# Gate, up and key-value products of an attention and mixture-of-experts block as three rounded products of split operands

## The chip, the cores and the metric

The kernel runs on one core of one Trainium2 chip. The metric is device microseconds of one launch, the median of several runs. The engines are TensorE (PE; PEld is its weight load), VectorE (DVE), ScalarE (ACT), GpSimd (POOL) and SyncE (SP), which issues most of the DMA.

## The reference

One block over x of 8 x 512 tokens of width 256: a modulated layer norm, multi-head latent attention with 16 heads, a gated residual, a second modulated norm, a shared gated feed-forward part of inner width 352, and 16 experts of inner width 176 with capacity 128 and top 4. Cut to what the change touches:

```python
h = _layernorm(x, axis=-1) * (1 + ca) + sa
fused = hidden @ w_kv_a                      # 192 query-latent, 64 key-latent, 64 rotary columns
...
h = _layernorm(x, axis=-1) * (1 + cb) + sb
scores = jax.nn.softmax(x @ gate_w.T, axis=-1)
topk_w, topk_i = jax.lax.top_k(scores, K)
...
shared = jax.nn.silu(x @ sw_gate) * (x @ sw_up) @ sw_down
```

All is f32.

## The kernel before

Eight batches of 512 tokens (4 tiles of 128) run in one loop. A batch has eight head pairs. `step` is one head pair: scores, exponentials, transposes of the probabilities, values, and the query projection of the next pair. Between two batches stands `middle(b, n, post, pre)`: `post` is the end of batch b (output projection, residual x1, second norm h2, shared feed-forward part, router), `pre` the start of batch n = b + 1 (key-value part, absorbed keys, first query projection). Seven of these have both halves; batch 0 starts with `pre` alone after the weights are prepared, and batch 7 ends with `post` alone, followed by the experts. Every engine has its own program, in an order written out by hand, and they meet at semaphores. GpSimd scatters routing entries, multiplies and adds the modulation of h2 (lines 494 and 496, behind a wait for the query rotation at line 493), and copies x.

The normed h1 is turned by TensorE (`turn_h1`, two halves of the width, both through bank 6 of the accumulator, the second after ScalarE has emptied the first). ScalarE writes hT with scale and bias (`turned_h1`, line 1043). The key-value part is `PS[t] = hT^T wkva_sb` for four tiles and two halves of the width (line 831), in the order 2, 0, 1, 3, each behind a wait for its bank. ScalarE then sums squares, GpSimd takes roots, VectorE scales into qn and kmat.

h2 is turned in two parts: three tiles (`turn_h2`, written by `turned_h2`, line 1050), then the last (`turn_h2_last`, `turned_h2_last`, line 1056). The inner width of the shared part is in three slices. The third slice, 96 columns, carries the 16 router columns too: `ffn_router` (lines 793 and 795), part 0 for the first 384 tokens and part 1 for the last 128. `ffn` (lines 781 and 783) computes gate and up of slices 0 and 1. `tanh_gate` on ScalarE and `silu_mid` on VectorE finish each slice.

The query projection and the scores already use split operands: a value is written once rounded to fp32r by ScalarE (high), VectorE subtracts that from the full value (low), and three products, high x high, low x high and high x low, are added in one bank (`scores`, lines 650 to 652; `q_project`; `q_low` at line 1262). The tiles hT, h2T, wkva_sb, sg_sb (gate and router columns) and su_sb (up) are f32.

## Time and profile before

| | us |
|---|---|
| median of 3 timed runs | 1249.4 |
| lowest, highest | 1245.29, 1251.21 |
| the profiled execution | 1254.99 |
| its span, first to last instruction | 1253.1 |

The profile is one execution. Its timelines give start and length in us, the engine, the line, what was written from what, and in square brackets how long the engine stood idle before and what released it. "x4" joins neighbouring records of the same form. A matmul's length holds a fixed latency and overlaps the next one, so its cost is the distance from one start to the next.

### The profile page before, as it was taken

The page shows a single profiled execution, that of the slowest core. Times are in us where ns is not written, and L with a number is a line of the kernel's source. Part 1 is how long each engine was busy: PE and PEld are TensorE (multiplying, and loading weights), DVE is VectorE, ACT ScalarE, POOL GpSimd, SP SyncE. Part 2 cuts the span into 40 slices and gives each one's busy share as a digit, 9 for nine tenths or more (in the row PEclk, how much of TensorE's full clock was granted, in tenths as well). Part 3 has the DMA queues.
Part 4 walks back from the last instruction along what each step waited for, and adds up shares of the span by engine and source line. Part 5 has one row for each costly group of instructions (what it writes and reads, how often), then busy time and mean ns, then how long its engine had stood idle before and what let it go on. Part 6 is the DMA issues. An engine that isn't in the chain of part 4 may idle for free.

```text
span 1253.1 us, 26074 instructions
## 1 busy us (share of the span) xinstructions
PE 1177.9 (94%) x7620; PEld 953.2 (76%) x7620; DVE 836.0 (67%) x2581; ACT 667.2 (53%) x1920; POOL 276.5 (22%) x332
## 2 busy tenths in 40 slices
PE   6799999999999999999999999999999999996782
PEld 3688778887888778887888778877888778873441
DVE  3677568776777667775877677766877577756221
ACT  2476626663567536763576447663667356731220
POOL 1000122211221122113212131212221122102553
PEclk9999999999999999999999999999999999997977
DMA  9410001000200001000100001000100010004752
GB/s 304 142 57 0 1 18 51 0 0 0 67 0 0 0 17 50 0 0 11 56 0 0 0 17 50 0 0 17 50 0 0 0 50 1 0 1 136 210 129 38
DMA packets 48317, 46.17 MB, mean 37 GB/s; under 512 B 10048, under 2 KB 44960, under 8 KB 48296
## 3 DMA queue, kind: packets, MB, share of 16 engines
q1 hardware_dynamic: 29096, 30.90, 8.1%
q0 software_dynamic: 7168, 6.37, 2.8%
q10 hardware_dynamic: 12032, 8.65, 2.4%
q8 instruction: 10, 0.16, 0.1%
q14 instruction: 11, 0.09, 0.0%
HBM read 35.04 MB, written 15.11 MB: 40 GB/s over the span
## 4 chain that ended last, share of the span: by engine, by line
PE 84%; DMA 5%; DVE 4%; issue 2%; ACT 2%; SPq 1%; POOL 1%; POOLq 0%; DVEq 0%; ACTq 0%
PE PS L671 11%; PE PS L692 10%; PE PS L802 8%; PE PS L650 7%; PE PS L651 6%; PE PS L652 6%; DMA out<-x_res,toku 5%; PE PS L636 4%; PE PS L810 4%; PE PS L831 3%; PE PS L623 3%; PE PS L626 2%; PE PS L627 2%; PE PS L624 2%; PE PS L625 2%; PE PS L781 2%
## 5 line engine op out<-in xcount | busy, mean ns | idle before, releaser
L987 ACT ACTIVATE probs<-probs,nmax 128x512 f32<-128x512 f32 (+3 forms) x512 | 283.0, 554 | 124.5 <-DVE nmax L1231 121.5
L1231 DVE CUSTOM_DVE_ANT_0 probs<-PS,cmask 128x512 f32<-128x512 f32 (+3 forms) x512 | 229.3, 488 | 98.6 <-PE PS L652 96.2
L540 POOL DMA_INDIRECT tab_dram<-entry,slot x112 | 110.5, 986 | 392.4 <-PE PS L692 371.1
L650 PE MATMUL PS<-kTh,qTh 128*128 128x512 f32 (+3 forms) x512 | 177.5, 347 | 1.7 <-DVE qTl L1262 1.5
L651 PE MATMUL PS<-kTl,qTh 128*128 128x512 f32 (+3 forms) x512 | 164.9, 322 | 0.0
L652 PE MATMUL PS<-kTh,qTl 128*128 128x512 f32 (+3 forms) x512 | 164.9, 322 | 0.0
L996 ACT ACTIVATE pT<-PS 128x384 f32<-128x384 f32 (+3 forms) x320 | 127.3, 462 | 70.6 <-PE PS L671 70.5
L671 PE MATMUL PS<-ident,probs 128*128 128x128 f32 x1280 | 164.8, 275 | 0.0
L692 PE MATMUL PS<-pT,kmat 128*64 128x512 f32 (+3 forms) x1024 | 151.9, 439 | 0.3 <-issue 0.3
L671 PEld LDWEIGHTS PS<-ident,probs 128*128 128x128 f32 x1280 | 141.4, 140 | 10.3 <-issue 7.4
L692 PEld LDWEIGHTS PS<-pT,kmat 128*64 128x64 f32 x1024 | 68.0, 136 | 76.0 <-issue 62.1
L802 PE MATMUL PS<-wvo,oT 128*128 128x256 f32 x512 | 116.4, 381 | 0.0
L1262 DVE TENSOR_TENSOR qTl<-PS,qTh 128x512 fp32r<-128x512 f32 x128 | 87.1, 685 | 34.0 <-ACT qTh L982 34.0
L650 PEld LDWEIGHTS PS<-kTh,qTh 128*128 128x128 f32 x512 | 96.5, 188 | 13.2 <-issue 4.6
L802 PEld LDWEIGHTS PS<-wvo,oT 128*128 128x128 f32 x512 | 95.4, 190 | 13.7 <-issue 1.4
L1248 DVE COPY pT<-PS 128x512 f32<-128x512 f32 (+2 forms) x192 | 81.5, 462 | 31.7 <-PE PS L671 31.4
L652 PEld LDWEIGHTS PS<-kTh,qTl 128*128 128x128 f32 x512 | 96.7, 189 | 5.4
L651 PEld LDWEIGHTS PS<-kTl,qTh 128*128 128x128 f32 x512 | 96.9, 189 | 4.9 <-issue 1.7
L987 ACT ACTIVATION_READ_ACCUMULATOR probs<-probs,nmax 128x1 f32 x512 | 95.7, 187 | 0.0
L1257 DVE TENSOR_TENSOR oT<-PS,th 128x512 f32 (+1 forms) x64 | 43.8, 684 | 51.0 <-PE PS L692 51.0
L623 PE MATMUL PS<-wq0h,ql0h 128*128 (+1 forms) x256 | 74.8, 292 | 2.1 <-DVE ql1s L1447 2.1
L626 PE MATMUL PS<-wq1hh,ql1s 128*128 (+1 forms) x256 | 72.4, 283 | 0.0
(242 smaller groups left out, 2084.9 us busy)
## 6 DMA issues: line engine op xcount, KB each, us to landing
x_in<-in_x SPq DMA_DIRECT2D x8, 512.0 KB, 5.9
modb<-mod_dram SPq DMA_DIRECT2D x8, 512.0 KB, 5.4
h_dram<-mod_dram SPq DMA_DIRECT2D x1, 4096.0 KB
h_dram<-h SPq DMA_DIRECT2D x8, 512.0 KB, 3.0
out<-base SPq DMA_DIRECT2D x8, 512.0 KB
pT<-in_wo SPq DMA_DIRECT2D x1, 2048.0 KB, 10.6
tab_dram<-entry,slot POOLq DMA_INDIRECT x112
oT<-in_wqnT SPq DMA_DIRECT2D x1, 1536.0 KB, 11.2
```

The lines of the kernel that those rows point to most:

```text
L540: pool.indirect_dma_start(tab_dram[:, :], bass.IndirectOffsetOnAxis(ap=slot[:, j:j + 1], axis=0), entry[:, j, :], None, bounds_check=NE * ...
L623: pe.matmul(dst, ql0h[:, tok], wq0h[:, cols], start=True, stop=False)
L626: pe.matmul(dst, ql1s[:, tok], wq1hh[:, cols], start=False, stop=False)
L650: pe.matmul(PS[:, bank, 0:n], qTh[:, h, rows_q], kTh[:, 0:n], start=True, stop=False)
L651: pe.matmul(PS[:, bank, 0:n], qTh[:, h, rows_q], kTl[:, 0:n], start=False, stop=False)
L652: pe.matmul(PS[:, bank, 0:n], qTl[:, h, rows_q], kTh[:, 0:n], start=False, stop=True).then_inc(s_ps, 1)
L671: mm = pe.transpose(PS[:, bank, col:col + P], probs[:, UO[u] + j * P:UO[u] + (j + 1) * P], ident[:])
L692: mm = pe.matmul(PS[h * KL:(h + 1) * KL, OBANK, j * P:S], kmat[:, j, 0:KL], pT[:, h, j, j * P:S], start=j == 0, stop=j == NT - 1)
L802: mm = pe.matmul(PS[:, bank, 0:H], oT[:, p, bass.ts(t, P)], wvo[:, p, :], start=p == 0, stop=p == NPAIR - 1)
L987: act.activation(probs[:, UO[u]:UO[u] + UW[u]], probs[:, UO[u]:UO[u] + UW[u]], ACT.Exp, scale=-1.0, bias=nmax[:, u:u + 1], accum_out=psums ...
L996: cp = act.activation(pT[:, h, 0:i + 1, bass.ts(i, P)], PS[:, bank, col:col + UW[u]].rearrange("p (j q) -> p j q", q=P), ACT.Copy)
L1231: dve.tensor_tensor_reduce(out=probs[:, UO[u]:UO[u] + UW[u]], in0=PS[:, SBANK[u], 0:UW[u]], in1=cmask[:, S - UW[u]:S], scale=-1.0, scalar= ...
```

## The change

Three groups of f32 products become three rounded products of split operands, added in the same bank: the key-value part of batches 1 to 7, gate and up of slices 0 and 1, and the first 384 tokens of the third slice with the router. The key-value part of batch 0 and the last 128 tokens of the third slice stay plain f32, from full copies of their operands (h1_full, wkva_st; h2_full[1], sg_r, su_r).

ScalarE writes each turned tile twice, full into tmp and rounded into hTh, and VectorE writes the difference hTl (`h1_low`, `h2_low`). hTh and hTl serve both h1 and h2. The last tile of h2 is written full first, then copied rounded. The second half of h1 is turned into bank 5, behind a wait for VectorE's values output, and ahead of probability groups 2 to 5. The weights are loaded into tiles that are free then (wkva_st in qtok, sg_st and su_st in midT, after the modulation has been stored) and split once, by ScalarE and VectorE, in the first `middle`. The loads of sg and su move behind SyncE's wait for that store, and two small loads (sg_r, su_r) are new. GpSimd waits for the modulation product before its first copy. Several tiles share storage to make room: kr1, kr2, xgT and emT lie in qr1 and qr2, and two of the expert row buffers are h2 instead of hT. The diff, cut to its core (the leading indentation is shortened):

```diff
@@ -238,7 +242,15 @@
-wm_st = [t[:].rearrange("p a n -> p (a n)").rearrange("p (c n) -> p c n", c=2) for t in (tmp, base, h2T)]
+wm_st = [t[:].rearrange("p a n -> p (a n)").rearrange("p (c n) -> p c n", c=2) for t in (tmp, base, x_res)]
+wkva_st = qtok[:].rearrange("p t n -> p (t n)")[:, 0:2 * FW].rearrange("p (c n) -> p c n", c=2)
+midT_flat = midT[:].rearrange("p a s -> p (a s)")
+sg_st = midT_flat[:, 0:2 * (IS + NE)].rearrange("p (c n) -> p c n", c=2)
+su_st = midT_flat[:, 2 * (IS + NE):2 * (IS + NE) + 2 * IS].rearrange("p (c n) -> p c n", c=2)
+turned = tmp[:].rearrange("p t n -> p (t n)")
+h1_full = turned.rearrange("p (c n) -> p c n", c=2)
+h2_full = (turned[:, 0:2 * (S - P)].rearrange("p (c n) -> p c n", c=2),
+       turned[:, 2 * (S - P):].rearrange("p (c n) -> p c n", c=2))
@@ -405,6 +424,10 @@
+sp.dma_start(sg_st, sgate.rearrange("(c p) n -> p c n", p=P)).then_inc(ffn_in, 16)
+sp.dma_start(su_st, sup.rearrange("(c p) n -> p c n", p=P)).then_inc(ffn_in, 16)
+sp.dma_start(sg_r[:], sgate.rearrange("(c p) n -> p c n", p=P)[:, :, MT[2][0]:]).then_inc(init_out, 16)
+sp.dma_start(su_r[:], sup.rearrange("(c p) n -> p c n", p=P)[:, :, MT[2][0]:]).then_inc(init_out, 16)
...
@@ -723,10 +747,9 @@
         turn_h1(b + 1, 0, 6)
-    turn_probs(g, first, (2, 3))
-    if last and more:
-        turn_h1(b + 1, 1, 6)
-    turn_probs(g, first, (4, 5))
+        pe.wait_ge(oT_ready, g + 1)
+        turn_h1(b + 1, 1, 5)
+    turn_probs(g, first, (2, 3, 4, 5))
     spread_sums(g)
...
@@ -777,23 +800,39 @@
     off, w = MT[m]
+    pe.wait_ge(h2Tl_ready, 2 * b + 2)
+    gate, up, m = PS[0:w, banks[0], :], PS[0:w, banks[1], :], slice(off, off + w)
     for c in range(2):
-        pe.matmul(PS[0:w, banks[0], :], sg_sb[:, c, off:off + w], h2T[:, c, :],
-                  start=c == 0, stop=c == 1)
-        mm = pe.matmul(PS[0:w, banks[1], :], su_sb[:, c, off:off + w], h2T[:, c, :],
-                       start=c == 0, stop=c == 1)
+        pe.matmul(gate, sg_h[:, c, m], hTh[:, c, :], start=c == 0, stop=False)
+        pe.matmul(gate, sg_l[:, c, m], hTh[:, c, :], start=False, stop=False)
+        pe.matmul(gate, sg_h[:, c, m], hTl[:, c, :], start=False, stop=c == 1)
+        pe.matmul(up, su_h[:, c, m], hTh[:, c, :], start=c == 0, stop=False)
+        pe.matmul(up, su_l[:, c, m], hTh[:, c, :], start=False, stop=False)
+        mm = pe.matmul(up, su_h[:, c, m], hTl[:, c, :], start=False, stop=c == 1)
     mm.then_inc(gu_ps, 1)
     off, w = MT[2]
-    lo, hi = (0, S - P) if part == 0 else (S - P, S)
+    mg, mu = slice(off, off + w + NE), slice(off, off + w)
+    if part:
+        gate, up = PS[0:w + NE, banks[0], S - P:S], PS[0:w, banks[1], S - P:S]
+        for c in range(2):
+            pe.wait_ge(h2T_ready, 4 * b + c + 3)
+            pe.matmul(gate, sg_r[:, c, :], h2_full[1][:, c, :], start=c == 0, stop=c == 1)
+            mm = pe.matmul(up, su_r[:, c, :], h2_full[1][:, c, :], start=c == 0, stop=c == 1)
+        return mm
+    gate, up, cols = PS[0:w + NE, banks[0], 0:S - P], PS[0:w, banks[1], 0:S - P], slice(0, S - P)
     for c in range(2):
-        pe.wait_ge(h2T_ready, 4 * b + 2 * part + c + 1)
-        pe.matmul(PS[0:w + NE, banks[0], lo:hi], sg_sb[:, c, off:off + w + NE], h2T[:, c, lo:hi],
-                  start=c == 0, stop=c == 1)
-        mm = pe.matmul(PS[0:w, banks[1], lo:hi], su_sb[:, c, off:off + w], h2T[:, c, lo:hi],
-                       start=c == 0, stop=c == 1)
+        pe.wait_ge(h2T_ready, 4 * b + c + 1)
+        pe.matmul(gate, sg_h[:, c, mg], hTh[:, c, cols], start=c == 0, stop=False)
+        pe.matmul(gate, sg_l[:, c, mg], hTh[:, c, cols], start=False, stop=False)
+        pe.matmul(up, su_h[:, c, mu], hTh[:, c, cols], start=c == 0, stop=False)
+        pe.matmul(up, su_l[:, c, mu], hTh[:, c, cols], start=False, stop=False)
+    pe.wait_ge(h2Tl_ready, 2 * b + 1)
+    for c in range(2):
+        pe.matmul(gate, sg_h[:, c, mg], hTl[:, c, cols], start=False, stop=c == 1)
+        mm = pe.matmul(up, su_h[:, c, mu], hTl[:, c, cols], start=False, stop=c == 1)
     return mm
...
@@ -817,20 +856,52 @@
+def key_values(n):
+    free = ((pT_act, 4 * n * NPAIR - 1), (pT_dve, 2 * n * NPAIR - 1),
+            (pT_act, 4 * n * NPAIR), (pT_dve, 2 * n * NPAIR))
+    def high(k):
+        t = KV_ORDER[k]
+        pe.wait_ge(*free[k])
+        for c in range(2):
+            pe.matmul(PS[:, t, 0:FW], hTh[:, c, bass.ts(t, P)], wkva_h[:, c, :],
+                      start=c == 0, stop=False)
+            pe.matmul(PS[:, t, 0:FW], hTh[:, c, bass.ts(t, P)], wkva_l[:, c, :],
+                      start=False, stop=False)
+    def low(k):
+        t = KV_ORDER[k]
+        for c in range(2):
+            mm = pe.matmul(PS[:, t, 0:FW], hTl[:, c, bass.ts(t, P)], wkva_h[:, c, :],
+                           start=False, stop=c == 1)
+        mm.then_inc(kv_ps, 1)
+    pe.wait_ge(wkval_ready, 1)
+    high(0)
+    high(1)
+    pe.wait_ge(hTl_ready, 2 * n)
+    low(0)
+    low(1)
+    high(2)
+    low(2)
+    high(3)
+    low(3)
 def middle(b, n, post, pre):
         if not post:
-            pe.wait_ge(wk_in, 4 * 16)
-        for k, t in enumerate(KV_ORDER):
-            if post:
-                pe.wait_ge(*((pT_act, 4 * n * NPAIR - 1), (pT_dve, 2 * n * NPAIR - 1),
-                             (pT_act, 4 * n * NPAIR), (pT_dve, 2 * n * NPAIR))[k])
-            for c in range(2):
-                mm = pe.matmul(PS[:, t, 0:FW], hT[:, c, bass.ts(t, P)], wkva_sb[:, c, :],
-                               start=c == 0, stop=c == 1)
-            mm.then_inc(kv_ps, 1)
+            pe.wait_ge(wkva_in, 16)
+        if post:
+            key_values(n)
+        else:
+            for t in KV_ORDER:
+                for c in range(2):
+                    mm = pe.matmul(PS[:, t, 0:FW], h1_full[:, c, bass.ts(t, P)], wkva_st[:, c, :],
+                                   start=c == 0, stop=c == 1)
+                mm.then_inc(kv_ps, 1)
     if post:
...
@@ -1015,8 +1088,10 @@
     elif more:
-        turned_h1(b + 1, (6, 6))
+        turned_h1(b + 1, (0,), 6)
     group_out(g, 2)
+    if last and more:
+        turned_h1(b + 1, (1,), 5)
     group_out(g, 4)
...
@@ -1035,26 +1110,32 @@
-def turned_h1(n, banks):
+def turned_h1(n, parts, bank):
     act.wait_ge(mod1_ready, n + 1)
-    for c in range(2):
+    for c in parts:
         act.wait_ge(hT_ps, 2 * n + c + 1)
-        act.activation(hT[:, c, :], PS[:, banks[c], :], ACT.Identity, scale=mod1[:, 2 + c:3 + c],
+        act.activation(h1_full[:, c, :], PS[:, bank, :], ACT.Identity,
+                       scale=mod1[:, 2 + c:3 + c], bias=mod1[:, c:c + 1])
+        act.activation(hTh[:, c, :], PS[:, bank, :], ACT.Identity, scale=mod1[:, 2 + c:3 + c],
                        bias=mod1[:, c:c + 1]).then_inc(hT_ready, 1)
         act.wait_ge(h2T_ps, 3 * b + c + 1)
-        act.activation(h2T[:, c, 0:S - P], PS[:, 1 + c, 0:S - P], ACT.Identity, scale=mod2[:, 2 + c:3 + c],
-                       bias=mod2[:, c:c + 1]).then_inc(h2T_ready, 1)
+        for dst in (h2_full[0][:, c, :], hTh[:, c, 0:S - P]):
+            cp = act.activation(dst, PS[:, 1 + c, 0:S - P], ACT.Identity, scale=mod2[:, 2 + c:3 + c],
+                                bias=mod2[:, c:c + 1])
+        cp.then_inc(h2T_ready, 1)
     for c in range(2):
-        act.activation(h2T[:, c, S - P:S], PS[:, 0, bass.ts(c, P)], ACT.Identity,
+        act.activation(h2_full[1][:, c, :], PS[:, 0, bass.ts(c, P)], ACT.Identity,
                        scale=mod2[:, 2 + c:3 + c], bias=mod2[:, c:c + 1]).then_inc(h2T_ready, 1)
+    act.wait_ge(h2T_ready, 4 * b + 4)
+    act.activation(hTh[:, :, S - P:S], h2_full[1], ACT.Copy).then_inc(h2Th_last, 1)
...
@@ -1076,9 +1157,15 @@
         turned_h2(b)
+    if not post:
+        act.activation(wkva_h[:], wkva_st, ACT.Copy).then_inc(wkvah_ready, 1)
+        act.wait_ge(wkval_ready, 1)
     if pre:
     if not post:
+        act.wait_ge(ffn_in, 2 * 16)
+        act.activation(sg_h[:], sg_st, ACT.Copy)
+        act.activation(su_h[:], su_st, ACT.Copy).then_inc(ffnh_ready, 1)
         act.wait_ge(wvo_ps, 1)
...
@@ -1456,10 +1546,20 @@
         normed(x1, h2, mv2, rstd2, range(3, 4), n2_ready)
+        h2_low(b, 0, slice(0, S - P))
+    if not post:
+        dve.wait_ge(wkvah_ready, 1)
+        dve.tensor_tensor(wkva_l[:], wkva_st, wkva_h[:].bitcast(F32),
+                          ALU.subtract).then_inc(wkval_ready, 1)
     if pre:
             part()
+    if post:
+        h2_low(b, 1, slice(S - P, S))
     if not post:
+        dve.wait_ge(ffnh_ready, 1)
+        dve.tensor_tensor(sg_l[:], sg_st, sg_h[:].bitcast(F32), ALU.subtract)
+        dve.tensor_tensor(su_l[:], su_st, su_h[:].bitcast(F32), ALU.subtract).then_inc(ffnl_ready, 1)
         dve.wait_ge(wvo_ps, 1)
...
@@ -1526,6 +1626,22 @@
+def h1_low(n):
+    for c in range(2):
+        dve.wait_ge(hT_ready, 2 * n + c + 1)
+        dve.tensor_tensor(hTl[:, c, :], h1_full[:, c, :], hTh[:, c, :].bitcast(F32),
+                          ALU.subtract).then_inc(hTl_ready, 1)
+def h2_low(b, part, cols):
+    if part:
+        dve.wait_ge(h2Th_last, b + 1)
+    else:
+        dve.wait_ge(h2T_ready, 4 * b + 2)
+    dve.tensor_tensor(hTl[:, :, cols], h2_full[part], hTh[:, :, cols].bitcast(F32),
+                      ALU.subtract).then_inc(h2Tl_ready, 1)
 def query_low(k):
```

Calls that go with it: `h1_low(b + 1)` stands on VectorE after the last probability copies of the last head pair; TensorE waits for ffnl_ready and init_out before the first `ffn_router` of each batch, which only the first can feel.

## Rows read from the trace of the kernel before

**Rows 1.** Table by stretch, 60 to 1104 us: length, busy by engine, clock, DMA.

```profile
core 0: us, PE busy (x) PEld busy (x) DVE busy (x) ACT busy (x) POOL busy (x), PEclk, DMA share, GB/s
60.00:1104.00 1044.00, 1036.79 (x6939) 861.01 (x6938) 755.02 (x2373) 619.69 (x1780) 216.02 (x259) 1.00 0.06 16
```

**Rows 2.** Timeline of PE, plain f32 products: start, length, engine, line, names, count.

```profile
149.12 4.57 PE L831 MATMUL PS<-wkva_sb,hT 128*128 128x320 f32 x16 [0.22 <-ACT pT L996]
...
153.62 2.37 PE L692 MATMUL PS<-pT,kmat 128*64 128x512 f32 x16
...
171.61 0.81 PE L793 MATMUL PS<-h2T,sg_sb 128*112 128x384 f32 x2
...
174.19 0.38 PE L774 MATMUL PS<-ident,h 128*128 128x128 f32 x2
...
176.96 1.02 PE L781 MATMUL PS<-h2T,sg_sb 128*128 128x512 f32 x2
177.82 1.02 PE L783 MATMUL PS<-h2T,su_sb 128*128 128x512 f32 x2
```

**Rows 3.** Timeline of PE, rounded products of scores and query projection.

```profile
184.60 0.39 PE L651 MATMUL PS<-kTl,qTh 128*128 128x512 f32 x1
184.83 0.40 PE L652 MATMUL PS<-kTh,qTl 128*128 128x512 f32 x1
...
186.19 0.28 PE L625 MATMUL PS<-wq0h,ql0l 128*128 128x256 f32 x1
186.31 0.28 PE L626 MATMUL PS<-wq1hh,ql1s 128*128 128x256 f32 x1
```

**Rows 4.** Timelines of PE, ACT and DVE, last head pair of batch 0.

```profile
145.63 0.66 PE L762 MATMUL PS<-ident,h 128*128 128x128 f32 x4 [0.20 <-DVE h L1185]
146.12 0.93 PE L671 MATMUL PS<-ident,probs 128*128 128x128 f32 x7
...
146.32 0.78 ACT L1043 ACTIVATE hT<-PS,mod 128x512 f32<-128x512 f32 x1 [0.20 <-PE PS L762]
...
146.06 0.68 DVE L1257 TENSOR_TENSOR oT<-PS,th 128x512 f32<-128x512 f32 x1
```

**Rows 5.** Timelines of ACT and DVE, stretch between batches 0 and 1.

```profile
170.29 1.23 ACT L1050 ACTIVATE h2T<-PS,mod 128x384 f32<-128x384 f32 x2 [6.27 <-PE PS L769]
...
174.61 0.81 ACT L1056 ACTIVATE h2T<-PS,mod 128x128 f32<-128x128 f32 x2 [2.20 <-PE PS L774]
...
172.15 0.42 DVE L1185 TENSOR_SCALAR h<-x,mv,rstd 128x256 f32<-128x256 f32 x1 [1.07 <-POOL rstd L473]
172.48 0.69 DVE L1210 TENSOR_TENSOR qr<-PS,cos_sb 128x512 f32<-128x512 f32 x1
...
173.86 0.69 DVE L1224 TENSOR_TENSOR qtok<-qr 128x512 f32<-128x512 f32 x1
```

**Rows 6.** Timeline of POOL in the same stretch.

```profile
174.85 2.36 POOL L494 TENSOR_TENSOR h<-h,modb 128x1024 f32<-128x1024 f32 x1 [2.74 <-PE PS L774]
177.29 2.37 POOL L496 TENSOR_TENSOR h<-h,modb 128x1024 f32<-128x1024 f32 x1
```

**Rows 7.** Instructions of line 1313: ns least/median/most, first and last start.

```profile
L1313 DVE TENSOR_SCALAR tsum<-tsum x8: 170/170/217, 190.1 to 1139.5; 128x4 f32<-128x4 f32 x8
```

**Rows 8.** Timeline of DVE and POOL, last batch.

```profile
1140.74 0.29 DVE L1323 TENSOR_TENSOR rest<-value,parts 128x128 f32<-128x128 f32 x1
...
1141.20 0.20 POOL L515 COPY before<-before 128x16 f32<-128x16 f32 x1
1141.38 0.37 DVE L1325 TENSOR_TENSOR parts<-rest,parts 128x128 bf16<-128x128 f32 x1
```

**Rows 9.** Timelines of DVE in the prologue and of PE in the last batch.

```profile
27.23 1.26 DVE L1533 SCALAR_TENSOR_TENSOR wq0l<-probs,qg_sb,wq0h 128x1024 fp32r<-128x1024 f32 x1
...
46.59 0.69 DVE L1224 TENSOR_TENSOR qtok<-qr 128x512 f32<-128x512 f32 x1
48.19 1.29 DVE L1465 COPY wvo<-PS 128x512 f32<-128x512 f32 x2 [0.90 <-PE PS L614]
...
1134.15 0.41 PE L817 MATMUL PS<-ident,lgT 16*128 16x16 f32 x4 [1.30 <-ACT lgT L1090]
```

More of the change, by code:

```diff
@@ L112, in adaln_block @@
         wvo = sb("wvo", [P, NPAIR, H])
-        wkva_sb = sb("wkva_sb", [P, 2, FW])
-        sg_sb = sb("sg_sb", [P, 2, IS + NE])
-        su_sb = sb("su_sb", [P, 2, IS])
+        wkva_h = sb("wkva_h", [P, 2, FW], F32R)
+        wkva_l = sb("wkva_l", [P, 2, FW], F32R)
+        sg_h = sb("sg_h", [P, 2, IS + NE], F32R)
+        sg_l = sb("sg_l", [P, 2, IS + NE], F32R)
+        su_h = sb("su_h", [P, 2, IS], F32R)
+        su_l = sb("su_l", [P, 2, IS], F32R)
+        sg_r = sb("sg_r", [P, 2, MT[2][1] + NE])
+        su_r = sb("su_r", [P, 2, MT[2][1]])
         sd_sb = sb("sd_sb", [P, 3, H])
@@ L139, in adaln_block @@
         tmp = sb("tmp", [P, NT, H])
-        hT = sb("hT", [P, 2, S])
-        h2T = sb("h2T", [P, 2, S])
+        hTh = sb("hTh", [P, 2, S], F32R)
+        hTl = sb("hTl", [P, 2, S], F32R)
         modT = sb("modT", [P, 8, B])
@@ L168, in adaln_block @@
         qr2 = sb("qr2", [P, 2 * NT, DR])
+        kr1, kr2 = qr1[:, 0:NT, :], qr2[:, 0:NT, :]
         qTh = sb("qTh", [P, 2, S], F32R)
@@ L219, in adaln_block @@
                                                                  qtok[:].rearrange("p t n -> p (t n)").bitcast(BF16))]
-        xg = [t[:].rearrange("p a n -> p (a n)")[:, k * 2 * H:(k + 1) * 2 * H] for t in (x_in, h1, hT, x1) for k in range(2)]
+        xg = [t[:].rearrange("p a n -> p (a n)")[:, k * 2 * H:(k + 1) * 2 * H] for t in (x_in, h1, h2, x1) for k in range(2)]
         ey = [x_res[:, i, :] for i in range(NT)]
@@ L223, in adaln_block @@
         ROWS_AHEAD = 6
-        xgT = sb("xgT", [P, 2, 2, P])
+        xgT = qr1[:].rearrange("p a d -> p (a d)").rearrange("p (q c s) -> p q c s", q=2, c=2)
         eth = sb("eth", [P, IM])
         emid = sb("emid", [P, 2, IM])
-        emT = sb("emT", [P, 2, 2, P])
+        emT = qr2[:].rearrange("p a d -> p (a d)").rearrange("p (q c s) -> p q c s", q=2, c=2)
         cT_sb = sb("cT_sb", [P, 2, B])
@@ L282, in adaln_block @@
         hT_ready = sem("hT_ready")
+        hTl_ready = sem("hTl_ready")
+        wkva_in = sem("wkva_in")
+        wkvah_ready = sem("wkvah_ready")
+        wkval_ready = sem("wkval_ready")
+        ffn_in = sem("ffn_in")
+        ffnh_ready = sem("ffnh_ready")
+        ffnl_ready = sem("ffnl_ready")
         kv_ps = sem("kv_ps")
@@ L314, in adaln_block @@
         h2T_ready = sem("h2T_ready")
+        h2Tl_ready = sem("h2Tl_ready")
+        h2Th_last = sem("h2Th_last")
         gu_ps = sem("gu_ps")
@@ L529, in _ @@
             roots_pre(0)
+            pool.wait_ge(mod_ps, 1)
             pool.wait_ge(x_landed, 16)
@@ L867, in middle @@
                     pe.wait_ge(x1_ready, 3 * b + 3)
+                    pe.wait_ge(ffnl_ready, 1)
+                    pe.wait_ge(init_out, 6 * 16)
                     ffn_router(b, 0, (3, 4))
@@ L1111, in query_high @@
                     act.activation(heads(high, lo, hi), src, ACT.Copy, scale=qg_sb[:, k:k + 1]).then_inc(wqh_ready, 1)
-            turned_h1(0, (6, 7))
+            turned_h1(0, (0,), 6)
+            turned_h1(0, (1,), 7)
             query_high(0)
@@ L1287, in step @@
                 group_out(g, 5)
+                if last and more:
+                    h1_low(b + 1)
                 if not last:
@@ L1432, in middle @@
                     ch.wait()
-                    dve.tensor_tensor(kmat[:, :, KL:], kr1[:], kr2[:], ALU.add).then_inc(k_ready, 1)
+                    dve.tensor_tensor(kmat[:, :, KL:], kr1, kr2, ALU.add).then_inc(k_ready, 1)
                 if post:
@@ L1537, in _ @@
             query_low(0)
-            dve.wait_ge(wk_in, 4 * 16)
+            dve.wait_ge(wk_in, 3 * 16)
             middle(0, 0, False, True)
```

6 lines of the change are left out of this document (1 added, 5 removed).

## The prediction

> **What bounds the kernel now.** I read the table of busy time by stretch first, then TensorE's own timeline, and last the timelines of the engines that feed it. From 60 to 1104 us, seven stretches between batches and the head pairs among them, TensorE is busy for 1036.79 of 1044.00 us at a granted clock of 1.00, the full 2.4 GHz; the next engine, VectorE, for 755.02 [rows 1]. So there the kernel goes at TensorE's pace, and a microsecond taken from TensorE is a microsecond of the whole, if the operands still come in time. The reader is to look for two things: what a product costs (from one record's start to the next one's), and how early each operand lies ready.
>
> **The products, one by one.** A plain f32 product stands in the trace as two records. At 512 columns two records take 177.82 - 176.96 = 0.86, so 0.43 us each [rows 2]. A rounded product (fp32r) is one record: 0.23 us at 512 columns and 0.12 at 256 [rows 3]; between them I read 0.148 for 320 columns and 0.175 for 384. Three rounded products thus cost 0.69 where one f32 product costs 0.86. Per batch:
> - key-value: 16 records from 149.12 to 153.62 = 4.50 us [rows 2]. After: 4 tiles x 2 x 3 = 24 x 0.148 = 3.55. Gain 0.95.
> - router, first 384 tokens: 8 records from 171.61 to 174.19 = 2.58 [rows 2]. After: 12 x 0.175 = 2.10. Gain 0.48. The last 128 tokens stay as they are.
> - gate and up, two slices: 8 x 0.43 = 3.44 each. After: 12 x 0.233 = 2.80. Gain 0.64 each, 1.28 together.
> Gross: 2.71 us per batch, 19.0 over the seven batches that have all of it.
>
> **What the new operands cost.** Each turned tile is now written twice by ScalarE (full and rounded), and VectorE subtracts one from the other. All of this is off TensorE, but TensorE waits for it at three places.
>
> First place, the last head pair (145 to 149 us). TensorE turns the first half of h1 from 145.63 and goes on at 146.12 [rows 4]. Now it waits there for VectorE's values output, which runs 146.06 to 146.74 [rows 4], since the second half goes to its bank; the 13 probability transposes and the spread of the sums stand behind that wait. Stall 0.65. ScalarE's chain: one write of 512 columns is 0.78 long [rows 4]; two writes of 384 columns, each 0.67 long, take 1.23 [rows 5], so they follow each other 0.1 sooner than their length, and I take 0.67 per further write of 512. From 146.32: two writes of the first half (to 147.66), the third probability group (to 148.3), two writes of the second half, done at 149.75. The key-value part waits for that: it starts at 149.75 instead of 149.12, 0.63 late, and ends at 149.75 + 3.55 = 153.30 instead of 153.62. VectorE's differences (0.69 each, the length of its 512-column add [rows 5]) are done at 150.75, and TensorE wants the first at 149.75 + 8 x 0.148 = 150.93: hidden, by 0.2. Left of the gain of 0.95: 0.32.
>
> Second place, the router. ScalarE starts at 170.29 [rows 5]. With four writes at 0.57 apart, the first rounded half is ready at 171.53 (TensorE wants it at 171.61) and the second at 172.67 (wanted at 172.31). Behind TensorE's wait stand the turn of the last tile and the query turn. VectorE must then finish the difference of 768 columns. Its length I read between 0.69 for 512 and 1.26 for 1024 columns [rows 5, 9]: 0.98. It is free at 172.57 [rows 5], starts at 172.72 and ends at 173.70; TensorE wants it at 172.70 + 4 x 0.175 = 173.40. So the router ends at 173.75 + 0.70 = 174.45 instead of 174.19: the gain of 0.48 becomes a loss of 0.26. On VectorE the query rotation, queued behind that difference, starts at 173.66 instead of 172.48 and ends at 175.73 instead of 174.55 [rows 5]; TensorE's query turn comes behind the router's end, after 176, and doesn't wait.
>
> Third place, gate and up of the first slice. They need the difference of the last 128 tokens. ScalarE's two writes (0.81 at 174.61 [rows 5], 0.26 later now) and the extra rounded copy end at about 176.15, and VectorE could then subtract in about 0.42 us, done at 176.6, while TensorE arrives at 176.96 + 0.26 = 177.2. That alone is hidden by 0.6. But GpSimd's multiply of h2 starts as soon as the query rotation is done (line 493), at about 175.85, and takes 2.36 us, followed at once by an add of 2.37 [rows 6]. The new difference reads both inputs from SBUF while GpSimd reads SBUF too, and nowhere in the trace of before does a long VectorE instruction of that kind stand beside one of GpSimd's. What little there is: a VectorE instruction on 4 columns takes 170 ns in the usual batch and 217 in the one where GpSimd works beside it, the last [rows 7]; of two VectorE subtractions of the same shape the one that begins while GpSimd copies takes 0.37 against 0.29 [rows 8]. They get in each other's way where they meet. The bounds: no stall at all, or the whole multiply. I take the whole multiply, since in these rows whichever came second is the longer: VectorE begins at 178.23, is done at 178.65, and TensorE starts at 178.7 instead of 177.2. Stall 1.5.
>
> The Trainium skill says the same more sharply ("SBUF — State Buffer", section "Who interferes with whom"): a VectorE instruction with two SBUF inputs contends with a GpSimd instruction that reads SBUF, and whichever issues first holds the shared ports for its whole length. No row of before shows it over such a length. By that rule the third place costs the stall of 1.5 us; without it nothing.
>
> **After that** the chain moves rigidly. VectorE's gate products start when ScalarE's tanh is done, and that follows TensorE's last product, so an earlier TensorE brings them forward with it; a VectorE delayed by 1.5 us at the third place has the whole first slice, 2.80, to catch up before its banks are wanted.
>
> **Sum per batch:** -0.32 + 0.26 + 1.5 - 1.28 = +0.16, over seven batches +1.1.
>
> **Ends.** Prologue: the twofold write of h1 moves the first key-value part by 0.3. The new splits of gate and up (736 and 704 columns) put two subtractions of about 0.84 each on VectorE ahead of its copies of the output weights, which began at 48.19 [rows 9] as TensorE delivered them. VectorE leaves the rotation at 47.6 (46.59 + 0.69 [rows 9] and the 0.3), the subtractions at 49.25; the copies, the query differences and the first scores come 0.75 later, the 0.3 included. ScalarE's two weight copies end at 47.0, before those weights are there, and cost nothing. The late loads are issued at about 34 us and needed at 45; were they late, each microsecond would be one of the whole. The key-value weights are split at 41 to 43, while TensorE projects queries: no cost. Last batch: no query work covers the router. The turned rows, the difference and the logits come 0.76 later (the logits' turn at 1134.15 already waits [rows 9]), and routing, the token table and the row updates that end the kernel hang on it; its faster gate and up lie beside VectorE's routing and give nothing. Together +1.5.
>
> **The sum against the profiled execution:** 1254.99 + 1.1 + 1.5 = 1257.6. That execution lies 5.6 above the median of the three timed runs, 1249.4; on the median the forecast is 1252.0. A difference below about 0.5% (6.2 us) can't be told from none by measuring this kernel.
>
> **Rivals.**
> - No contention: the 128-column difference is done at 176.6 and hidden. Per batch -1.34, over seven -9.4, with the ends -7.9: 1241.5. For it: the marks in [rows 7, 8] are small, 0.05 to 0.08 us.
> - All hand-overs hidden, or my waits too long: the gross gain counts, about -19: 1230.4. Against it: the write chains are sums of measured lengths.
> - The change doesn't do what it says, if rounded products of these shapes went at the f32 record's pace: 24 x 0.43 = 10.3 for gate and up against 6.9 now, 3.4 us per batch more. [rows 3] speak against it; I fold it into the slower side.
>
> **Chances.** Forecast 0.52, no contention 0.33, blocked twice or a costlier product 0.08, all hidden 0.07. Each case carries some 3 us either way from the estimated lengths. No contention lies beyond the 0.5% bound in two of three cases: 0.22, with all hidden 0.29 faster. Of the forecast 0.08 lies above the bound, with the slower case 0.16 slower. Within: 0.55. The range takes in the two likely cases with their spread, 1238 to 1260; the likeliest case alone would be 1248 to 1256.
>
> **What would show it.** In the profile after: 168 rounded key-value records (7 x 24) about 0.148 us apart; TensorE idle of 0.65 before the second turn of h1 on VectorE's values output; idle of 0.3 to 0.4 before the router's second half; and above all a difference of the last 128 tokens on VectorE about 2 us long, or starting when GpSimd's multiply ends, with TensorE idle about 1.5 us before the first gate product. If that idle is absent, the forecast is wrong and the first rival holds. If TensorE's idle over the batches grows by under 2 us in all, the last but one does.

## The result, and the profile after

The changed kernel takes 1254.81 us (median of 7 runs, 1253.38 to 1256.98), the kernel before on the same chip 1250.83 (7 runs): ratio 1.004 over all runs (1.0032 between the two medians), 95% interval 1.0022 to 1.0058. So it is slower by 0.4%, inside the bound of 0.5% of "no change" and 2.8 us above the forecast of 1252.0. The profiled execution took 1256.25 us.

The page of the changed kernel, its span and busy times:

```profile
span 1253.5 us, 26510 instructions
...
PE 1165.1 (93%) x7772; PEld 974.5 (78%) x7772; DVE 870.3 (69%) x2614; ACT 692.7 (55%) x1963; POOL 277.4 (22%) x332
```

Its table by stretch, the columns as in [rows 1]:

```profile
60.00:1104.00 1044.00, 1020.97 (x7082) 876.02 (x7081) 786.83 (x2407) 641.04 (x1818) 216.84 (x259) 1.00 0.06 16
```

TensorE worked 15.8 us less between 60 and 1104 us than in [rows 1] (1036.79), at the same full clock, and VectorE 31.8 more. The time didn't fall, so TensorE idled more. Its waits say where (engine, bank, line, what released it: us in total, times, longest):

```profile
PE PS L806 <- DVE hTl L1642: 7.4, 7, 1.1
PE PS L822 <- ACT tmp L1135: 4.4, 8, 0.5
...
PE PS L868 <- ACT hTh L1120: 3.8, 7, 0.5
...
PE PS L785 <- DVE oT L1345: 3.6, 7, 0.5
```

L822, the last 128 tokens of the router, waited as long in the kernel before. The other three come once in each of seven batches: before the first gate product (L806) and before the second turn of h1 (L785), where the kernel before didn't wait, and before the first key-value product (L868), where it waited 0.22 [rows 2] and now waits 0.54. TensorE's timeline of the same batch as [rows 2 to 4]:

```profile
148.89 0.66 PE L785 MATMUL PS<-ident,h 128*128 128x128 f32 x4
150.06 0.66 PE L785 MATMUL PS<-ident,h 128*128 128x128 f32 x4 [0.52 <-DVE oT L1345]
...
153.11 0.41 PE L868 MATMUL PS<-wkva_h,hTh 128*128 128x320 f32 x1 [0.54 <-ACT hTh L1120]
...
175.06 0.40 PE L828 MATMUL PS<-hTh,sg_h 128*112 128x384 f32 x1
...
176.16 0.43 PE L828 MATMUL PS<-hTh,sg_h 128*112 128x384 f32 x1 [0.17 <-ACT hTh L1128]
...
181.93 0.50 PE L806 MATMUL PS<-hTh,sg_h 128*128 128x512 f32 x1 [1.06 <-DVE hTl L1642]
182.27 0.39 PE L807 MATMUL PS<-hTh,sg_l 128*128 128x512 f32 x1
```

**How I compare.** An execution starts its batches up to 4 us earlier or later than another of the same kernel (below). Between batches 0 and 1, the same points agree within 0.03 us in every profiled execution of the same kernel. So all times below count from the first turn of h1 in the last head pair (145.63 before [rows 4], 148.89 here):

| from the first turn of h1 | before | predicted | after |
|---|---|---|---|
| first key-value product | 3.49 | 4.12 | 4.22 |
| values (end of key-value) | 7.99 | 7.67 | 7.93 |
| turn of the keys | 15.58 | 15.26 | 15.73 |
| router, first half | 25.98 | 25.66 | 26.17 |
| router's end | 28.56 | 28.50 | 29.05 |
| first gate product | 31.33 | 32.77 | 33.04 |
| second score product after gate and up | 38.97 | 39.13 | 39.52 |

Against before that is +0.55 us per batch, where the forecast has +0.16. One line of the table needs a second look: the values begin 0.06 earlier than before, but the turn of the keys 0.15 later. ScalarE's first square, GpSimd's root, the last write of kmat and the turn of the keys, before and then after:

```profile
150.50 0.33 ACT L1063 ACTIVATE sq<-PS 128x192 f32<-128x192 f32 x1 [0.57 <-PE PS L831]
...
154.98 1.66 POOL L473 TENSOR_TENSOR ssq<-ssq,mhalf 128x8 f32<-128x8 f32 x1
...
160.36 0.42 DVE L1433 TENSOR_TENSOR kmat<-kr 128x256 f32<-128x256 f32 x1
...
161.21 0.60 PE L849 MATMUL PS<-ident,kmat 128*128 128x128 f32 x4
```

```profile
154.87 0.33 ACT L1144 ACTIVATE sq<-PS 128x192 f32<-128x192 f32 x1 [1.04 <-PE PS L876]
...
158.76 1.66 POOL L496 TENSOR_TENSOR ssq<-ssq,mhalf 128x8 f32<-128x8 f32 x1
...
164.14 0.42 DVE L1523 TENSOR_TENSOR kmat<-qr 128x256 f32<-128x256 f32 x1
...
164.62 0.66 PE L920 MATMUL PS<-ident,kmat 128*128 128x128 f32 x4
```

Before, kmat lay ready 0.43 us ahead of its turn (160.78, 161.21). Now TensorE turns it 0.06 after it is done (164.56, 164.62).

The third place, on VectorE and on GpSimd, in the same execution:

```profile
179.64 2.23 DVE L1642 TENSOR_TENSOR hTl<-tmp,hTh 128x256 fp32r<-128x256 f32 x1 [0.56 <-ACT hTh L1138]
```

```profile
179.23 2.36 POOL L517 TENSOR_TENSOR h<-h,modb 128x1024 f32<-128x1024 f32 x1 [3.66 <-DVE qtok L1312]
181.67 2.50 POOL L519 TENSOR_TENSOR h<-h,modb 128x1024 f32<-128x1024 f32 x1
```

VectorE's difference of the last 128 tokens, 256 elements wide, takes 2.23 us. GpSimd's multiply had begun 0.41 earlier, and the difference ends 0.28 after it. The idle of 1.06 in TensorE's row is counted from the end of a record that overlaps the next one; from start to start the way from the router's end to the gate product has grown by 1.22 (3.99 against 2.77).

### The profile page after: what moved, and what is told of

It is laid out like the page before. It is cut to its first block, busy times and chain, and to the rows that moved or that the text cites. A ratio compares the mean times of both kernels' runs of the same rounds, so it can differ in the third digit from the quotient of the medians.

```text
span 1253.5 us, 26510 instructions
## 1 busy us (share of the span) xinstructions
PE 1165.1 (93%) x7772; PEld 974.5 (78%) x7772; DVE 870.3 (69%) x2614; ACT 692.7 (55%) x1963; POOL 277.4 (22%) x332
## 4 chain that ended last, share of the span: by engine, by line
PE 75%; DVE 7%; DMA 6%; issue 5%; ACT 4%; POOL 2%; SPq 1%; POOLq 0%; DVEq 0%; ACTq 0%
PE PS L695 11%; PE PS L716 9%; PE PS L674 6%; PE PS L675 6%; PE PS L676 6%; PE PS L841 5%; DMA out<-x_res,toku 5%; PE PS L660 4%; PE PS L849 3%; PE PS L647 2%; PE PS L650 2%; PE PS L651 2%; PE PS L648 2%; PE PS L649 2%; PE PS L705 2%
## 5 line engine op out<-in xcount | busy, mean ns | idle before, releaser
L674 PE MATMUL PS<-kTh,qTh 128*128 128x512 f32 (+3 forms) x512 | 171.9, 336 | 1.5 <-DVE qTl L1350 1.5
L1336 DVE COPY pT<-PS 128x512 f32<-128x512 f32 (+2 forms) x192 | 78.0, 460 | 11.6 <-PE PS L695 11.6
L651 PE MATMUL PS<-wq1l,ql1s 128*128 (+1 forms) x256 | 72.9, 285 | 0.0
```

The source lines that it names most:

```text
L651: mm = pe.matmul(dst, ql1s[:, tok], wq1l[:, cols], start=False, stop=True)
L674: pe.matmul(PS[:, bank, 0:n], qTh[:, h, rows_q], kTh[:, 0:n], start=True, stop=False)
```

## The experiments

Each ratio is against the kernel before on the same chip. The last columns set two measures side by side: the sum of the seven stretches from the spread of the sums in a batch's seventh pair to that in the next batch's first pair, less that of before (445.4 us in two executions), and the timed difference (ratio less one, times the median of before).

| kernel | ratio, interval | 7 stretches, us | less before | timed |
|---|---|---|---|---|
| changed kernel | 1.0040, 1.0022 to 1.0058 | 449.31 | +3.9 | +5.0 |
| e0 the same again | 1.0048, 1.0031 to 1.0065 | 449.43 | +4.0 | +6.0 |
| e1 GpSimd waits | 0.9967, 0.9951 to 0.9983 | 439.97 | -5.4 | -4.1 |
| e2 GpSimd only writes | one run | 439.91 | -5.5 | |
| e3 batch 0 full only | 1.0035, 1.0022 to 1.0048 | 449.38 | +4.0 | +4.4 |
| e4 second turn later | one run | 448.15 | +2.8 | |
| e5 rounded copy first | 1.0017, 1.0004 to 1.0030 | 447.73 | +2.3 | +2.1 |
| e6 e1 and e5 together | 0.9931, 0.9911 to 0.9951 | 438.35 | -7.0 | -8.7 |
| e7 key-value plain | 1.0022, 1.0009 to 1.0035 | 448.34 | +2.9 | +2.8 |
| e8 router plain | 1.0039, 1.0024 to 1.0054 | 449.25 | +3.9 | +4.9 |
| e10 gate and up only | 0.9935, 0.9916 to 0.9953 | 436.85 | -8.5 | -8.2 |
| e11 all but the router | 0.9893, 0.9873 to 0.9913 | 433.00 | -12.4 | -13.4 |

The two agree within 2 us everywhere, which is about the width of the intervals, so within that what the change costs and what the experiments give back lies in these seven stretches. That is the main reading of the study.

**e0, the changed kernel once more.**

> The changed kernel itself, unaltered, so that the other runs of this call have it beside them on the same chip. Expected 3 to 5 us above the kernel before. Theory P (the prologue is slower because TensorE is left at 1.2 GHz there by the added work ahead of it) expects the first turn of h1 in the last head pair of batch 0 again at about 148.9 us, 3.3 later than before, and a granted clock of 0.50 over the first query projection. Theory C (the clock in the prologue is chance, one execution has it and another not) expects that mark anywhere between 146.4 and 149.

Measured: 1261.54 us, ratio 1.0048. The times inside the batch are those of the table within 0.03. The first turn of h1 stands at 146.92, 2 us earlier than in the execution above, with a clock of 0.64 instead of 0.50 over 42 to 48 us: the prologue differs between executions of one kernel.

**e1, GpSimd's multiply waits for the difference.**

```
 wait_alone(pool, rope_ready, n * NPAIR + 1)
+pool.wait_ge(h2Tl_ready, 2 * b + 2)
 pool.tensor_tensor(h2[:], h2[:], spread(2), ALU.mult)
```

> The changed kernel, with GpSimd's multiply of h2 in batches 0 to 6 held back until VectorE has written the difference of the last 128 tokens. Nothing is left out. Theory A (the two instructions exclude each other because both read SBUF, and GpSimd had it first): the difference of 256 columns falls from 2.23 us to about 0.42, TensorE's idle before the first gate product (7.4 us in all) goes to under 1 us, and the time falls by 7 times 1.06 = 7.4 us against the changed kernel, to about 3.4 below the kernel before. Theory B (the length in the trace is a wait for ScalarE's rounded copy or for a semaphore, not a conflict): length and idle stay, and the time is that of the changed kernel within 1 us, or worse by the later GpSimd work.

Measured: 1251.75 us, 9.8 below e0. VectorE, GpSimd and TensorE:

```profile
179.24 0.43 DVE L1643 TENSOR_TENSOR hTl<-tmp,hTh 128x256 fp32r<-128x256 f32 x1 [0.57 <-ACT hTh L1139]
```

```profile
179.84 2.41 POOL L518 TENSOR_TENSOR h<-h,modb 128x1024 f32<-128x1024 f32 x1 [4.69 <-DVE hTl L1643]
```

```profile
180.22 0.48 PE L807 MATMUL PS<-hTh,sg_h 128*128 128x512 f32 x1
```

The same instruction takes 0.43 us instead of 2.23, TensorE's idle before the gate product is gone, and that product (line 807 here) comes at 31.75 instead of 33.04, 1.29 earlier. Theory A is right and B is refuted. The seven stretches give back 9.3 us, more than the 7.4 expected, since I had counted the idle of 1.06 and not the distance of starts. One wait on GpSimd, whose work isn't urgent here, turns the change from 0.4% slower into 0.3% faster than before.

**e2, GpSimd writes the same bytes but reads nothing.** This leaves out the scaling of h2 in batches 0 to 6, so the experts' rows aren't the reference's.

```
-pool.tensor_tensor(h2[:], h2[:], spread(2), ALU.mult).then_inc(h2_scaled, 1)
+for k in range(NT):
+    zero = pool.memset(h2[:, k, :], 0.0)
+zero.then_inc(h2_scaled, 1)
```

> The changed kernel, with GpSimd's multiply of h2 in batches 0 to 6 replaced by four fills of h2 with zeros, so that the experts' rows are wrong: GpSimd writes SBUF over the same stretch but reads nothing. Theory A1 (only GpSimd's reads stand against a VectorE instruction with two SBUF inputs): the difference of 256 columns is 0.42 us long although it falls into the fills. Theory A2 (any GpSimd instruction does): it ends only when the fills end, or after the one it met, so it is 0.7 us or longer.

GpSimd and VectorE, then the difference by its line (duration in ns: least, median, longest):

```profile
177.86 1.07 POOL L519 MEMSET h<- 128x256 f32 x4 [3.63 <-DVE qtok L1317]
```

```profile
178.31 0.43 DVE L1647 TENSOR_TENSOR hTl<-tmp,hTh 128x256 fp32r<-128x256 f32 x1 [0.57 <-ACT hTh L1143]
```

```profile
L1647 DVE TENSOR_TENSOR hTl<-tmp,hTh x16: 424/958/1452, 174.8 to 1130.2; 128x768 fp32r<-128x768 f32 x8, 128x256 fp32r<-128x256 f32 x8
```

The difference lies wholly inside GpSimd's four writes (177.86 to 178.93) and takes 0.43; the seven stretches are as in e1 (439.91). The fills aren't held up either: four of them, 0.31 us each with an overlap, take 1.07 in all, so VectorE didn't just slip in between two of them. So GpSimd's writing alone doesn't hold VectorE; its multiply, which reads SBUF (the memory of the tiles) too, does. The longest, 1.452, is that of the last batch, which keeps the multiply:

```profile
1128.97 2.35 POOL L522 TENSOR_TENSOR h<-h,modb 128x1024 f32<-128x1024 f32 x1 [2.98 <-PE PS L802]
...
1130.15 1.45 DVE L1647 TENSOR_TENSOR hTl<-tmp,hTh 128x256 fp32r<-128x256 f32 x1 [2.56 <-ACT hTh L1143]
```

The difference begins 1.18 into the multiply and ends 0.28 after it. The length of the difference is set by when the multiply ends.

**e3, batch 0 writes only the full copy of h1.**

```
-act.activation(h1_full[:, c, :], PS[:, bank, :], ...)
+full = act.activation(h1_full[:, c, :], PS[:, bank, :], ...)
+if isinstance(n, int):
+    full.then_inc(hT_ready, 1)
+    continue
 act.activation(hTh[:, c, :], PS[:, bank, :], ...)
```

> The changed kernel, without ScalarE's rounded write of h1 for batch 0, which no product of batch 0 reads. Nothing of the result is left out. My theory has the first key-value products 0.3 us earlier and the rest of the prologue by as much, so 0 to 0.5 us below the changed kernel, which this timing can hardly tell. Theory P (this added work leaves TensorE at the low clock) expects 2 to 3 us less, the granted clock over the first query projection back at 1.00 and the first turn of h1 in the last head pair near 146.4.

Measured: 1260.48 us, 1.1 below e0, within the uncertainty. Clock 0.50 over 42 to 48 us and the turn of h1 at 149.05: taking the second write away doesn't bring the clock back.

**e9, the kernel before once more.**

> The kernel before once more, unchanged, with a profile: it asks whether the half clock of the prologue belongs to the change. Seen so far, one execution each: TensorE over its first query projection (42 to 48 us) at a granted clock of 1.00 in the kernel before, and at 0.50 to 0.83 in the executions of the changed kernels; the first turn of h1 in the last head pair then stands at 145.6 before and at 145.9 to 149.2 in the others. Theory C (the clock in the prologue differs by chance from execution to execution): this execution may show 0.5 to 0.8 over 42 to 48 us too, and then the turn of h1 stands at 147 to 149. Theory P (the change's longer prologue causes it): clock 1.00 over 42 to 48 us and the turn at 145.3 to 146. One execution can refute P but not C. Within the batch nothing is left to chance: turn of h1 to router 25.98 (within 0.03), to the second score product 38.97.

Over 42 to 45 us, the table by stretch of this execution, then that of the profiled execution of before (columns as in [rows 1]; the clock is the third number from the end):

```profile
42.00:45.00 3.00, 2.20 (x10) 2.23 (x11) 0.66 (x1) 0.00 (x0) 0.00 (x0) 0.50 0.41 99
```

```profile
42.00:45.00 3.00, 3.00 (x26) 2.72 (x28) 0.00 (x0) 0.43 (x1) 0.00 (x0) 1.00 0.26 90
```

The kernel before, too, can have its first query projection at 1.2 GHz; the turn of h1 then stands at 149.22, later than in the changed kernel. Theory P is refuted. All times inside the batch are those of before, to 0.01 us.

**e4, the second turn of h1 behind two more groups of transposes.**

```
-if last and more: wait oT_ready; turn_h1(b + 1, 1, 5)
-turn_probs(g, first, (2, 3, 4, 5))
+turn_probs(g, first, (2, 3))
+if last and more: wait oT_ready; turn_h1(b + 1, 1, 5)
+turn_probs(g, first, (4, 5))
```

> The changed kernel, with the turn of the second half of h1 (and TensorE's wait for VectorE's values output in front of it) put behind probability groups 2 and 3 again. Theory A (ScalarE's chain of doubled writes ends last there): the stall of 0.52 us before the turn goes, but the idle before the first key-value product grows by as much, from 0.54 to about 1.06, and the stretch from the first turn of h1 to the start of the values, 7.93 us, stays within 0.1. Theory B (TensorE's wait is the cost): that stretch falls by 0.5 us in each of seven batches.

The wait of 0.52 for VectorE's values output is gone, and TensorE waits 1.12 instead of 0.54 before the first key-value product, for ScalarE. The values begin at 7.77 instead of 7.93, a little outside the 0.1 of Theory A and far from the 0.5 of Theory B. Left: 0.15 per batch (router at 26.03). The stall had been cover for ScalarE's chain.

**e5, the rounded copy first, the full one second** (and none rounded in batch 0).

```
-act.activation(h1_full...); act.activation(hTh...).then_inc(hT_ready, 1)
+act.activation(hTh...).then_inc(hT_ready, 1)
+act.activation(h1_full...).then_inc(hTf_ready, 1)
```

The same for h2 with h2T_ready and h2Tf_ready; VectorE waits for the full copies.

> The changed kernel, with ScalarE's two writes of each turned tile in the other order: the rounded one first, which TensorE waits for, then the full one, which only VectorE needs; and without the rounded write of batch 0, which nothing reads. Nothing of the result is left out. If ScalarE's chain ends last at both places, the key-value part starts 0.5 to 0.7 us earlier, the squares and with them the keys too, so that TensorE's idle before the turn of the keys (0.25) goes, and the router's second half no longer waits 0.35: in all 1.0 to 1.3 us per batch less than the changed kernel, 7 to 9 us. If VectorE's differences end last instead, these waits only move behind the high products and it gains under 0.3 per batch.

Measured: 1.0017, about 3 us better than the changed kernel and 0.23 per batch in the seven stretches. That is the second case of the expectation (under 0.3 per batch), not the 7 to 9 us of the first. TensorE:

```profile
151.08 0.86 PE L878 MATMUL PS<-wkva_h,hTl 128*128 128x320 f32 x4 [0.17 <-DVE hTl L1638]
...
173.97 0.43 PE L836 MATMUL PS<-hTl,sg_h 128*112 128x384 f32 x1 [0.52 <-DVE hTl L1647]
```

The first key-value product comes at 3.56 instead of 4.22, and the router's second half doesn't wait. But the difference needs both copies, so both waits come back ahead of the products that read it: the router takes 2.87 as before the edit (2.88), and the turn of the keys stands at 15.52, 0.21 earlier.

**e7, key-value plain, h1 written once** (16 f32 products from h1_full and a full wkva).

> The changed kernel with the key-value part of all batches in plain f32 again, from the full copy alone: no rounded write of h1, no difference, no split of those weights, all else as changed (the turn into bank 5 too). Nothing of the result is left out. The two records per product cost 0.8 us more per batch, the waits before and behind that stand at 0.54 and 0.25 go: the stretch from the first turn of h1 to the router stays within 0.2 us of the changed kernel's 26.17, so the key-value part in rounded products is worth about nothing. If instead the waits were small change, the stretch would grow by 0.6 or more and the time by 4 us.

Values at 8.06, turn of the keys at 15.65, router at 26.04: 0.13 per batch better than with the rounded products. In the changed kernel the 24 rounded products bring nothing.

**e8, the router's first 384 tokens plain.**

> The changed kernel with the router and the third slice in plain f32 for all tokens, from the full copy that ScalarE now writes first for both halves; the rounded copies and the difference follow for the other two slices. Nothing of the result is left out. Expected: the router's stretch falls from 2.88 us to 2.58, as before the change, 0.3 per batch, and about 0.8 in the last batch, where routing hangs on it: 2 to 3 us less in all. If the rounded products there were worth their count, it would be 0.5 per batch slower instead.

The router takes 2.58 instead of 2.88 as expected, but the gate product comes at 33.06 as in the changed kernel (33.04). VectorE, GpSimd and TensorE:

```profile
179.11 2.53 DVE L1638 TENSOR_TENSOR hTl<-tmp,hTh 128x256 fp32r<-128x256 f32 x1 [0.27 <-ACT hTh L1134]
```

```profile
178.98 2.37 POOL L518 TENSOR_TENSOR h<-h,modb 128x1024 f32<-128x1024 f32 x1 [3.66 <-DVE qtok L1308]
```

```profile
181.69 0.50 PE L807 MATMUL PS<-hTh,sg_h 128*128 128x512 f32 x1 [1.36 <-DVE hTl L1638]
```

The difference starts 0.27 earlier and takes 0.30 longer; it ends 0.29 after GpSimd's multiply, and TensorE idles 1.36 instead of 1.06. My error was to count a gain ahead of a wait whose end doesn't depend on it. In the last batch, where routing hangs on the router and not on the gate product, the logits' turn does come 0.74 earlier (22.98 after the last spread of the sums, 23.72 in e0); the timing can't tell that from nothing.

**e6, e1 and e5 together.**

> Two edits on the changed kernel: GpSimd's multiply of h2 waits for the difference of the last 128 tokens, and ScalarE writes the rounded copies before the full ones (and none in batch 0). Measured from the first turn of h1 in the last head pair: router at 25.98 and its end at 28.85 (as with the order of writes alone), then 2.69 to the first gate product and 6.45 to the second score product (as with the GpSimd wait alone): 37.99, against 38.97 before and 39.52 in the changed kernel. If the two gains add up: -0.98 per batch against before, -6.9 in all, with about +1 to +2 of the ends a ratio of 0.995 to 0.997. If the gain of the order of writes falls into another wait once GpSimd is out of the way: 38.2, as with the GpSimd wait alone, ratio 0.9967.

Measured: 0.9931, second score product at 37.96 (37.99 expected). The gains add up: 9.3 and 1.6 us of the seven stretches alone, 11.0 together.

**e10, gate and up only** (e1, e7 and e8 together).

> Only gate and up of the slices keep the three rounded products: key-value and the router's first 384 tokens go back to plain f32, h1 is written once, and GpSimd's multiply waits for the difference of the last 128 tokens. Theory D (rounding pays here only where its operands are hidden; the key-value and router parts gain nothing): turn of h1 to router 26.0, router 2.58, then 2.69 and 6.45: second score product at 37.75, that is -1.2 per batch against before, -8.5 in all; with cheaper ends a ratio of 0.993 to 0.995, the fastest of all. Rival K (the key-value part in rounded products does gain something once the rest is hidden): slower than the kernel with both edits, ratio 0.996 or more.

Measured: 0.9935, second score product at 37.74 (37.75 expected). With GpSimd out of the way the plain router's 0.30 counts: against e1 the stretches fall by 3.1 us, of which e7 explains 1.0.

**e11, all but the router** (e1, e4, the h1 part of e5, and e8). Its text says that both turns of h1 move; only the second one does.

> As the one before, but with key-value in three rounded products and everything done to hide its operands: rounded copy written first, and the two turns of h1 moved behind the second group of probability transposes. Theory D: the key-value part ends 0.3 to 0.5 earlier, but the turn of the keys that follows waits for kmat, whose chain (ScalarE's squares 0.88 per tile, GpSimd's root, VectorE) starts with the first finished tile; so the turn of keys stands at 15.4 to 15.6 as before (15.58), the second score product at 37.6 to 37.8, and the time within 1.5 us of the gate-and-up-only kernel. Rival K: turn of keys at 15.2 or less, score product at 37.4 or less, and 2 us or more faster than the gate-and-up-only kernel.

Measured: 1241.51 us, 0.9893, and 6.0 faster than e10, of which 3.9 lie in the seven stretches and the rest is within the spread of the timing. Rival K is right: turn of the keys at 15.05, second score product at 37.21. ScalarE's first squares and TensorE's turn of the keys in e6, then in e11:

```profile
152.22 0.33 ACT L1150 ACTIVATE sq<-PS 128x192 f32<-128x192 f32 x1 [0.81 <-PE PS L879]
```

```profile
161.97 0.66 PE L923 MATMUL PS<-ident,kmat 128*128 128x128 f32 x4
```

```profile
150.31 0.33 ACT L1148 ACTIVATE sq<-PS 128x192 f32<-128x192 f32 x1 [0.52 <-PE PS L875]
```

```profile
160.06 0.66 PE L919 MATMUL PS<-ident,kmat 128*128 128x128 f32 x4
```

161.97 - 152.22 and 160.06 - 150.31 are both 9.75, and the same distance stands in the changed kernel, e4 and e5. I had the chain right (squares at 0.88 a tile, GpSimd's root, VectorE's scaling, kmat) but took it as fixed in the batch. It hangs on the first finished key-value tile, and that comes 0.45 earlier from the first turn of h1 than in e6 (5.30 against 5.75). Besides, TensorE doesn't wait before the second turn. Each of the two edits alone left its gain in the other's wait: e4 had 0.15 and the order of writes 0.21 a batch; with the plain router's 0.30 that would be 0.66 against e1, and e11 has (439.97 - 433.00) / 7 = 1.00.

## Why the prediction was nearly right

The time fell inside the range and its sign was in the likeliest class. Each step:

- **Third place, the deciding one: right.** Predicted: the difference is held by GpSimd's multiply until the multiply ends, stall 1.5; measured 1.22 more from router's end to gate product than before (3.99 against 2.77), and 1.29 more than without the hold (33.04 against 31.75 in e1). e1 and e2 show the cause by taking the multiply away in time and then its reads. The rival "no contention" is refuted by 2.23 against 0.43 us; "blocked twice" by the difference's end at 181.87, 0.28 after the multiply's, while the add, begun at 181.67, went on to 184.17. The rule that stood beside this step in the prediction (the Trainium skill, "SBUF — State Buffer", section "Who interferes with whom") holds here over a whole instruction: GpSimd's multiply came first wherever the two met, and VectorE's difference was done only 0.28 after its end, 1.8 us later than the 0.43 it takes alone. The other order, the multiply begun while the difference runs, stands in no run.
- **First place: wrong.** Predicted -0.32, measured +0.19 at the router. Two terms were a little small: the start 0.73 late instead of 0.63, and 3.71 us for the 24 products instead of 3.55. What failed is the sentence "Left of the gain of 0.95: 0.32", which took an earlier end of key-value for an earlier batch. Behind it stands ScalarE's chain of squares. In the rounded order the first tile is finished only after 10 of 24 products (before: after 2 of 8), so the squares start at 5.98 instead of 4.87 and end at 9.39 instead of 8.87; the tiles follow each other at ScalarE's own 0.88 now, and followed TensorE's products at 1.08 before. kmat had 0.43 of slack before (ready at 15.15, turned at 15.58); now TensorE waits for it, at 15.73. e5 shows this apart from the two small terms: its values begin at 7.72, nearly the predicted 7.67, and its keys are turned at 15.52, not at the predicted 15.26. No step of the prediction followed that chain. This place is off by 0.51 of a batch, more than the whole error.
- **Router: right.** +0.26 predicted, 2.88 against 2.58 measured, +0.30; e8 takes it back exactly. That it weighed nothing in the changed kernel, since the gate product waited for GpSimd's multiply whether the router was late or not, wasn't predicted.
- **Gate and up:** 1.16 gained instead of 1.28. The first product of each slice takes 0.34 instead of 0.23 (0.32 in e1, where no wait stands before it); before, only that of the second slice was longer (0.97 against 0.86).
- **Sum:** 0.19 + 0.30 + 1.22 - 1.16 = +0.55 per batch, +3.9 over seven, instead of +1.1.
- **Last batch: right.** From the last spread of the sums to the logits' turn 22.98 before, 23.72 in e0, e1, e3 and e6, and 22.98 again with the router plain (e8, e10, e11): +0.74 where 0.76 was predicted. In the profiled execution of the changed kernel it is 24.59, at a granted clock of 0.55 over the router.
- **Prologue: not found.** +0.75 was predicted, 0.3 of it for the twofold write of h1 ahead of the first projection and the rest for VectorE's subtractions. Compared at the same clock (e9 against the changed kernel, both 0.50), the first projection begins at 42.80 before and 42.71 after (it comes up to 1.9 us earlier in other executions of the same kernel, 40.84 in e0), and from there to the first scores it takes 11.40 before and 11.31 after. At full clock no execution of the changed kernel shows it, so for that case it stays open.
- Of "what would show it": 24 rounded records per batch 0.147 apart, as said; idle before the second turn 0.52 on VectorE's values output (0.65 said; from start to start it is 0.68, 1.17 between the two turns less the 0.49 of the first); idle before the router's second half (0.3 to 0.4 said): 0.40 (1.10 from the first half's start to the second's, less four products of 0.175).

That the predicted 1252.0 lies only 2.8 us under the measured time is partly luck: the error in the batches (+2.8) and the prologue's missing 0.75 stand against each other, and the median of before moved by 1.4 us when measured again.

## What to carry to other kernels

Cheaper products on the bounding engine pay only where the operands that they need come from engines with room at that place: here gate and up paid as soon as GpSimd waited (e10), key-value paid clearly only with the write order and the turn changed together (turn of the keys at 15.64 when plain in e10, 15.50 with the write order alone in e6, 15.05 in e11; whether it needs the GpSimd wait as well, no run shows), and the router never did (2.88 in rounded products, 2.58 in plain ones). When a new VectorE instruction with two SBUF inputs stands near a long GpSimd instruction that reads SBUF too, delay the GpSimd one by a wait if nobody needs it soon. Follow each product's result to its next reader on another engine, and ask when the first tile of it is ready, not when the last one is.

## What the runs showed that I had not expected

- The prologue's clock is a matter of the execution: over 42 to 48 us 0.50 to 1.00 in the fourteen executions profiled, in the kernel before 1.00 and 0.50. The first turn of h1 moves roughly with it from 145.0 to 149.2, in the kernel before from 145.63 to 149.22. What sets it is open.
- A head pair in the middle of a batch takes between 12.15 and 12.5 us in the same kernel. Of the first six intervals between spreads of the sums in each batch, 48 in all, 41 took at most 12.21 in the changed kernel's profiled execution, and 8 in e0. The 49 intervals outside the seven stretches sum to 598.35 there, 603.59 in e0 and 603.80 and 604.34 in the two executions of before. That is why the change's span looked unchanged (1253.5 against 1253.1) although each batch was 0.55 longer. The cause is open; comparing spans of single executions would have misled me by 5 us.
